# A hand-ordered opening and first turn for a two-layer graph attention kernel

## The reference

```python
# layer 0, for each graph (8 heads of 32)
nx = ln(x, ln1_g, ln1_b)
q, k, v = nx @ wq + bq, nx @ wk + bk, nx @ wv + bv
bias = where(adj > 0, 0.1 * edge * adj, -inf)          # edge is adj itself
attn = softmax(q k^T / sqrt(32) + bias)
x1 = x + (attn v) @ wo + bo
x2 = x1 + gelu(ln(x1, ln2_g, ln2_b) @ w1 + b1) @ w2 + b2   # hidden 1024, exact gelu
# layer 1, for each graph (one head of 256)
sc = (x2 @ Wq)(x2 @ Wk)^T / sqrt(256), -inf where adj == 0
y = x2 + softmax(sc) (x2 @ Wv) @ Wo + bo
out = ln(y, gamma, beta)
```

## Time and profile before

| | us |
|---|---|
| median of 3 runs (lowest, highest) | 935.13 (934.89, 935.47) |
| the profiled execution's own time | 935.03 |
| its span, first to last instruction | 933.3 |
| TensorE busy in the span | 903.3 |
| VectorE, ScalarE, GpSimd busy | 691.0, 641.2, 388.6 |
| mean granted TensorE clock | 0.993 |

### The profile page before, as it was taken

One profiled execution on the slowest core, in us unless ns is written; L12 is line 12 of the kernel. 1 busy time (PEld: TensorE's weight loads), 2 busy tenths in 40 slices (PEclk: granted clock), 3 DMA queues, 4 the chain that ended last, 5 costly groups with the idle time before them and its releaser, 6 DMA issues.

```text
span 933.3 us, 22588 instructions
## 1 busy us (share of the span) xinstructions
PE 903.3 (97%) x7623; PEld 805.8 (86%) x7623; DVE 691.0 (74%) x2576; ACT 641.2 (69%) x1888; POOL 388.6 (42%) x257
## 2 busy tenths in 40 slices
PE   8889999999999999999999999999999999998995
PEld 8677798988889898888989888898988889898894
DVE  7676877869587786958779595877968687786745
ACT  5675958668496766858677585866758586685751
POOL 3425153543616354262535526263451626344221
PEclk9999999999999999999999999999999999999998
DMA  7101000010101001010100101010010100000001
GB/s 260 35 1 35 2 24 24 30 29 0 56 0 34 22 22 34 0 51 6 34 22 22 34 0 35 22 34 22 22 34 0 34 22 28 11 24 1 24 1 34
DMA packets 29727, 26.29 MB, mean 28 GB/s; under 512 B 1126, under 2 KB 29436, under 8 KB 29692
## 3 DMA queue, kind: packets, MB, share of 16 engines
q1 hardware_dynamic: 29676, 25.83, 8.8%
q10 hardware_dynamic: 16, 0.00, 0.0%
HBM read 17.44 MB, written 8.39 MB: 28 GB/s over the span
## 4 chain that ended last, share of the span: by engine, by line
PE 43%; issue 21%; DVE 15%; POOL 14%; ACT 6%; POOLq 1%; DVEq 0%; ACTq 0%
PE bank L327 10%; PE bank L329 9%; PE bank L328 9%; DVE nx L1083 4%; POOL x L1519 4%; DVE hT_lo L1009 3%; PE bank L471 3%; POOL y L1524 3%; PE bank L564 3%; PE bank L592 3%; ACT bank L829 2%; PE bank L463 2%; POOL adj_s L1468 2%; POOL bias L1477 2%; POOL rstd L1450 2%
## 5 line engine op out<-in xcount | busy, mean ns | idle before, releaser
L804 ACT ACTIVATE bank<-p_s,neg_max 128x128 f32<-128x128 f32 x512 | 182.2, 356 | 24.1 <-DVE neg_max L1112 23.9
L1450 POOL TENSOR_TENSOR rstd<-ve,minus_half 128x4 f32<-128x4 f32 (+1 forms) x51 | 54.9, 1077 | 312.8 <-DVE ve L1076 312.8
L327 PE MATMUL bank<-w_hi,hT_hi 128*128 128x256 f32 x512 | 147.4, 288 | 0.0
L329 PE MATMUL bank<-w_hi,hT_lo 128*128 128x256 f32 x512 | 144.1, 282 | 0.0
L328 PE MATMUL bank<-w_lo,hT_hi 128*128 128x256 f32 x512 | 144.1, 281 | 0.0
L1112 DVE CUSTOM_DVE_ANT_0 p_s<-bank,bias 128x128 f32<-128x128 f32 x512 | 112.5, 285 | 8.4 <-PE bank L463 8.3
L327 PE MATMUL bank<-n2T_hi,w_hi 128*128 128x512 f32 (+1 forms) x272 | 110.1, 405 | 3.4 <-DVE qk_lo L1010 3.3
L829 ACT ACTIVATE bank<-bank,vec_cols 128x512 f32<-128x512 f32 (+1 forms) x136 | 86.6, 637 | 30.5 <-PE bank L329 30.5
L329 PE MATMUL bank<-n2T_hi,w_lo 128*128 128x512 f32 (+1 forms) x272 | 104.0, 382 | 0.0
L328 PE MATMUL bank<-n2T_lo,w_hi 128*128 128x512 f32 (+1 forms) x272 | 103.8, 382 | 0.0
L327 PEld LDWEIGHTS bank<-w_hi,hT_hi 128*128 128x128 f32 x512 | 96.4, 188 | 2.5 <-DVE hT_lo L1009 0.8
(11 more groups left out here) (211 smaller groups left out, 2460.4 us busy)
## 6 DMA issues: line engine op xcount, KB each, us to landing
xs<-in_x SPq DMA_DIRECT2D x15, 512.0 KB, 3.7
out<-y SPq DMA_DIRECT2D x15, 512.0 KB, 2.9
adj_i<-in_adj SPq DMA_DIRECT2D x15, 256.0 KB, 2.8
x2T_f<-in_L_gnn_w SPq DMA_DIRECT2D x1, 512.0 KB, 7.0
tT<-in_L_gnn_w SPq DMA_DIRECT2D x1, 512.0 KB, 7.8
y<-in_L_gnn_w SPq DMA_DIRECT2D x1, 512.0 KB, 6.4
vo<-in_L_gnn_w SPq DMA_DIRECT2D x1, 512.0 KB, 7.8
x_bo<-in_x SPq DMA_DIRECT2D x1, 256.0 KB, 2.8
```

The lines of the kernel that those rows point to most:

```text
L327: mm(out, a_hi, b_hi, start=first, stop=False)
L329: return mm(out, a_lo, b_hi, start=False, stop=last)
L804: last = run(bank[r][:, NODES * place:NODES * place + NODES], p_s[:, r, place, :], ACT.Exp, scale=-1.0, bias=neg_max[:, r, place:place + 1 ...
L1450: P.tensor_tensor(t["rstd"][:, 0:k], t["ve"][:, 0:k], minus_half[:, 0:k], ALU.pow).then_inc(ln_pool[n], 1)
```

## The change

All three engines get an order of their own for the opening, and `first_turn` in place of `turn(2, 1, 0)`. No arithmetic operation is added or dropped; `l1_product` is cut into its two halves (4 matmuls each). The hidden tiles of group 0 stand two in a bank (`up_place`), and ScalarE and VectorE take them in the order 0, 2, 1, 3, 4, 6, 5, 7 (`hidden`), a tile only once both of its bank are written. `HIGH` and `LOW` number the split weights in the order in which ScalarE and VectorE now finish them. The banks of `nx`, `n2`, `v` and the layer 1 transposes change for groups 0 and 1, and the waits with them. GpSimd's and SyncE's lists are not touched.

```diff
+        def hidden(g, i):
+            return (0, 2, 1, 3, 4, 6, 5, 7)[i] if isinstance(g, int) and g == 0 else i
+        def up_place(g, j):
+            if isinstance(g, int) and g == 0:
+                return bank[up_bank[j // 2]][:, D * (j % 2):D * (j % 2) + D]
+            return bank[at("up", g)[j % 4]][:, toks(g)]
...
+            def gelu(g, i):
+                j = hidden(g, i)
+                if isinstance(g, int) and g == 0:
+                    act.wait_ge(pe_up, 2 * (j // 2) + 2)
+                    if j % 2:
+                        act.wait_ge(dve_h, i - 1)
...
# project_v: bank 6 for both pairs of group 1
+                if isinstance(g, int) and g == 1:
+                    pe.wait_ge(*((act_k, 4), (dve_h, 7))[q])
# mlp_up of group 0
+                    if j == 4:
+                        pe.wait_ge(act_v, 2)
+                    elif j == 6:
+                        pe.wait_ge(dve_lo, LOW["qk1"])
...
# TensorE, the opening
             shift_bo()
+            norm_transpose(1)
             shifts_up()
-            l1_transpose(0)
-            norm_transpose(1)
-            l1_transpose(1)
-            p_transpose(0, 0)
-            attend(0, 0)
-            l1_transpose(2)
-            out_project(0, 0)
             project_k(1, 0)
             project_k(1, 1)
-            n2_transpose(0, False, False)
+            l1_transpose(0)
+            p_transpose(0, 0)
+            l1_transpose(1)
+            attend(0, 0)
             project_q(1, 0)
+            out_project(0, 0)
             project_q(1, 1)
+            l1_product(0, 0)
             scores(1, 0)
             project_v(1, 0)
-            project_v(1, 1)
-            l1_product(0)
-            turn(2, 1, 0)
+            n2_transpose(0, False, False)
+            l1_product(0, 1)
+            first_turn()
...
# TensorE, first_turn
+                pe.wait_ge(dve_lo, LOW["w1"])
+                for j in range(HT):
+                    mlp_up(0, j, True)
+                p_transpose(1, 0)
+                attend(1, 0)
+                out_project(1, 0)
+                l1_transpose(2)
+                scores(1, 1)
+                project_v(1, 1)
+                pe.wait_ge(dve_lo, LOW["w2"])
+                mlp_down(0, 0)
+                norm_transpose(2)
+                l1_product(1, 0)
+                l1_product(1, 1)
+                project_v(2, 0)
+                x2_transpose(0)
+                project_k(2, 0)
+                p_transpose(1, 1)
+                project_k(2, 1)
+                attend(1, 1)
+                t_project(0)
+                out_project(1, 1)
+                project_q(2, 0)
+                project_q(2, 1, True)
+                scores1(0, True)
+                scores(2, 0)
+                n2_transpose(1, True, True)
+                pe.wait_ge(dve_s1, 1)
+                project_v(2, 1)
+                vo_project(0, 0, True)
+                p1_transpose(0)
+                attend1(0)
...
# ScalarE, the opening
             exps(0, 0, 0)
             v_copy(0, 0)
-            for r in range(1, HPT):
-                exps(0, 0, r)
+            exps(0, 0, 1)
+            nxT_copy(1)
+            exps(0, 0, 2)
+            exps(0, 0, 3)
+            k_copy(1, 0)
+            k_copy(1, 1)
             pT_copy(0, 0, 0)
-            nxT_copy(1)
             pT_copy(0, 0, 2)
+            l1_copy(0, "wq1")
             l1_copy(1, "wk1")
             attn_high(0, 0)
             high_w1()
-            l1_copy(2, "wv1")
-            high_w2()
-            k_copy(1, 0)
-            k_copy(1, 1)
-            n2T_copy(0)
             q_copy(1, 0)
             q_copy(1, 1)
+            high_w2()
             exps(1, 0, 0)
+            n2T_copy(0)
+            layer1_high(0)
             exps(1, 0, 1)
             v_copy(1, 0)
-            v_copy(1, 1)
             exps(1, 0, 2)
             exps(1, 0, 3)
-            layer1_high(0)
...
# ScalarE, first_turn
+                gelu(0, 0)
+                pT_copy(1, 0, 0)
+                pT_copy(1, 0, 2)
+                gelu(0, 1)
+                gelu(0, 2)
+                attn_high(1, 0)
+                for j in range(3, HT):
+                    gelu(0, j)
+                run(probe[:, :], minus_half[:, 0:1], ACT.Exp)
+                v_copy(1, 1)
+                exps(1, 1, 0)
+                exps(1, 1, 1)
+                nxT_copy(2)
+                exps(1, 1, 2)
+                layer1_high(1)
+                exps(1, 1, 3)
+                x2T_copy(0)
+                x2T_high(0)
+                pT_copy(1, 1, 0)
+                pT_copy(1, 1, 2)
+                v_copy(2, 0)
...
+                exps1(0)
+                n2T_copy(1)
+                exps(2, 0, 0)
+                v_copy(2, 1)
+                exps(2, 0, 1)
+                vo_copy(0)
+                p1T_copy(0)
+                exps(2, 0, 2)
+                exps(2, 0, 3)
...
# VectorE, the opening
             moments(1, 1)
+            low_wo()
             biased(0, 0, 0)
             shift_v()
-            for r in range(1, HPT):
-                biased(0, 0, r)
+            biased(0, 0, 1)
+            norm1(1)
+            biased(0, 0, 2)
+            biased(0, 0, 3)
             shift_bo()
-            low_wo()
-            norm1(1)
-            divided(0, 0, 0)
+            nxT_low(1)
             shifts_up()
-            divided(0, 0, 1)
-            divided(0, 0, 2)
-            divided(0, 0, 3)
+            for r in range(HPT):
+                divided(0, 0, r)
             pT_copy(0, 0, 1)
             pT_copy(0, 0, 3)
-            l1_copy(0, "wq1")
-            nxT_low(1)
+            low_w1(0)
             attn_low(0, 0)
-            low_w1(0)
+            low_w1(1)
             residual1(0, 0, False)
             sums2(0, 0)
             moments(2, 0)
+            low_w2(0)
             norm2(0)
-            low_w1(1)
+            biased(1, 0, 0)
+            biased(1, 0, 1)
             n2T_low(0)
-            for r in range(HPT):
-                biased(1, 0, r)
-            divided(1, 0, 0)
-            low_w2(0)
-            divided(1, 0, 1)
-            divided(1, 0, 2)
-            low_w2(1)
-            divided(1, 0, 3)
-            l1_low(0, "qk1", qk1_p, SCALE1)
-            turn(2, 1, 0, None)
+            l1_low(0, "qk1", qk1_p, SCALE1)
+            biased(1, 0, 2)
+            biased(1, 0, 3)
+            low_w2(1)
+            first_turn()
...
# VectorE, first_turn
+                divided(1, 0, 0)
+                divided(1, 0, 1)
+                sums1(2)
+                divided(1, 0, 2)
+                divided(1, 0, 3)
+                moments(1, 2)
+                h_low(0, 0)
+                pT_copy(1, 0, 1)
+                pT_copy(1, 0, 3)
+                h_low(0, 1)
+                h_low(0, 2)
+                attn_low(1, 0)
+                h_low(0, 3)
+                h_low(0, 4)
+                residual1(1, 0, True)
+                sums2(1, 0)
+                l1_copy(2, "wv1")
+                for j in range(5, HT):
+                    h_low(0, j)
+                biased(1, 1, 0)
+                norm1(2)
+                for r in range(1, HPT):
+                    biased(1, 1, r)
+                residual2(0, 0)
+                divided(1, 1, 0)
+                nxT_low(2)
+                divided(1, 1, 1)
+                l1_low(1, "vo1", vo1_p, 1.0)
+                divided(1, 1, 2)
+                x2T_low(0)
+                divided(1, 1, 3)
+                pT_copy(1, 1, 1)
+                pT_copy(1, 1, 3)
...
```

More of the change, by code:

```diff
@@ L368, in shift_bo @@
                 for t in range(KT):
-                    last = mm(bank[4][:, 0:D], bv_cols[:, t, :], raw["wo"][:, t, :], start=(t == 0), stop=(t == KT - 1))
+                    last = mm(bank[5][:, 0:D], bv_cols[:, t, :], raw["wo"][:, t, :], start=(t == 0), stop=(t == KT - 1))
                 last.then_inc(pe_shift, 1)
@@ L389, in l1_transpose, with l1_product @@
                 last.then_inc(pe_l1, 1)
-            def l1_product(k):
+            def l1_product(k, m):
                 if k == 0:
+                    pe.wait_ge(act_l1, 2)
+                else:
                     pe.wait_ge(dve_l1, 1)
[L394 to L397, removed]
                 n, rhs = (("wq1", l1_T["wk1"]), ("wv1", raw["wo1"]))[k]
[L399 to L403, removed]
+                for c in range(KT):
+                    last = mm(bank[l1_mm_bank[k]][:, D * m:D * m + D], l1_T[n][:, c, 128 * m:128 * m + 128],
+                              rhs[:, c, :], start=(c == 0), stop=(c == KT - 1))
+                if m == KT - 1:
+                    last.then_inc(pe_l1_mm, 1)
             def norm_transpose(g):
-                if isinstance(g, int) and g == 1:
-                    pe.wait_ge(act_v, 1)
-                    pe.wait_ge(dve_shift, 8)
+                if isinstance(g, int) and g == 2:
+                    pe.wait_ge(act_v, 3)
                 pe.wait_ge(ln_dve[1], ln_end(g))
@@ L435, in project_q @@
```

(27 more changed lines are left out.)

104 lines of the change are left out of this document (56 added, 48 removed).

## The result

The changed kernel takes 942.62 us (median of 4 executions, 942.08 to 944.96), the kernel before 935.18 on the same chip: a ratio of 1.0084, 95% interval 1.0067 to 1.0102. It is slower, as forecast, but by 7.4 us and not by 2.4, and the time lies outside the range that I gave.

What follows compares the result with a forecast made beforehand. TensorE, busy 97% of the span, bounds the kernel; only the second turn's start can move. Opening and first turn shift it from 96.40 to 98.8 us, +2.4 on 935.03: median forecast 937.5 us, range 932.4 to 939.8.

Steps and rivals of the forecast that it cites:

- The order of the low part of the first weight ahead of `attn_low`: Opening, VectorE: `low_w1(0)` waits for `high_w1` with `attn_low(0, 0)` queued behind; TensorE stands 3.35 us ahead of `out_project(0, 0)`.
- the wait for `qk_lo`: First turn: TensorE's 3.3 us wait ahead of the fourth hidden tile goes, with about 1.6 us of slow matmuls.
- the two tiles in a bank: First turn: ScalarE waits 0.7 us for the second tile before the first `gelu`, hidden by the table load: nothing.
- the moved `low_wo`: Opening: `low_wo` fits in VectorE's 1.5 us wait for the first scores, needing 0.7 us: nothing.
- the load of group 2's `x`: First turn: it lands at about 51 us, `sums1(2)` reads it at 52.9; a cover 2 us thin.
- 1.1 us (`v(1, 1)`): First turn: `v(1, 1)` waits for low parts of hidden tiles queued behind `residual1`, `sums2` and an `l1_copy`: 1.1 us.
- 2.1 (`attend1`): End of first turn: two `exps` and a `v_copy` precede `vo_copy` and `p1T_copy`; `attend1(0)` waits 2.1 us instead of 0.4.
- I take the fall, lasting as long as the one at 52 us: Behind the wait ahead of `out_project(0, 0)`: half clock for some 3.4 us, costing 1.5 us more.
- Rival 3: A further clock fall between 42.9 and 47.8 us slows the tiles and transposes; with late `x`, 939.5 us; chance 0.12.
- Rival 2: First turn: eight tiles cover the softmax, saving 2.8 us of waits, and 1.5 with a held clock: 933.2 us; chance 0.18.

Runs made afterwards that it cites:

- a2: The changed kernel with 12 matmuls on the identity, into an unread bank, in the wait ahead of `out_project(0, 0)`: ratio 1.0044 to the kernel before.
- the repeat: The changed kernel unedited, measured and profiled a second time with more executions: ratio 1.0079 to the kernel before; the profiled execution took 940.71 us.
- b1: The kernel before with `low_w1(0)` ahead of `attn_low(0, 0)` on VectorE, nothing else: 941.09 us, ratio 1.0063.
- a6: The changed kernel with `attn_low(0, 0)` before `low_w1(0)`, `low_w2(0)` later, `vo_copy(0)`, `p1T_copy(0)` before `exps(2, 0, 1)`, `exps(1, 1, 2)` before `nxT_copy(2)`: ratio 1.0016.
- a7: a6 with VectorE's four `divided(1, 0, .)` in one piece, the `w2` splits and `sums1(2)` behind them, `h_low` right behind `residual1`: 934.21 us, ratio 0.9966.
- a9: a7 with `low_w1(0)` put back ahead of `attn_low(0, 0)` on VectorE, nothing else: 936.97 us, ratio 1.0001.

## Why the prediction was right or wrong

**What held.** What bounds the kernel: everything lies ahead of the second turn. The middle is untouched but for 0.9 us that came back behind the second turn's transposes; the earlier trace rows allowed for 2.2 there. The order of the low part of the first weight ahead of `attn_low` is the largest single price: the wait was forecast at 3.35 us and is 3.20, and the start of `out_project` after the first scores at 22.2 and is 22.9. Removed and free, as forecast: the wait for `qk_lo`, the two tiles in a bank, the moved `low_wo`, the load of group 2's `x`. The waits that I priced at 1.1 us (`v(1, 1)`) and 2.1 (`attend1`) measured 1.0 and 2.0. Ahead of the first hidden tile the forecast left TensorE 3.6 us without work (42.9 to 47.8, less 1.3), and it had 3.0 (0.89 and 2.15). Where the clock did as I assumed, up to `attend(1, 0)`, the count was short by 0.7 us of 45; 0.4 of it is `k(1)`, which had the clock at half for 3.4 us (24.3 to 27.7) where I had 2.6.

**What failed is one step, the number of falls.** "I take the fall, lasting as long as the one at 52 us" gives the sum one fall behind a wait, that ahead of `out_project(0, 0)`; every other wait is priced at its own length, as if none could bring the clock down. That fall came, and two came behind it that have no term in the sum. The missing 5.1 us (942.6 less 937.5) are, by the table: 0.8 in the start of the first scores; 0.7 up to `attend(1, 0)`; 1.5 more up to `mlp_down`, with the twelve `wo` matmuls at half clock (62.03 to 64.54) and, on the way, ScalarE's last `gelu` waiting 3.3 us for `h_low(0, 5)` behind that late residual; 1.8 more up to the second turn, of which 1.1 to `q(2, 1)` is in small parts that I can't name one by one, and 0.4 is `attend1` at half clock; 1.2 in the second turn's first tiles; less 0.9 given back. What the two falls cost can be read against a2, whose profile has neither: 9.9 us against 8.7 from `attend(1, 0)` to `mlp_down`, 1.2 against 0.8 in `attend1`, 7.0 against 5.8 from there to the transposes. That is 2.8 us. The other 2.4 us up to the transposes are my count, short nearly everywhere, where the prediction allowed it 1.2 either way. Rival 3, a further fall, was the right mechanism with the wrong place (ahead of the first tiles, where the tiles hide it, as a2 and the second profile show). Its 0.12 was little: both profiles of the changed kernel have a costly fall at a later wait.

**Why the falls are many.** The kernel before has one long wait (3.3 us) and short ones around it. The changed kernel has seven of 1.0 to 3.2 us. With the first of them filled and the order as it was (a2) about half of the loss is gone; the repeat shows that which wait brings the clock down changes from one execution to the next with the waits themselves fixed. That more waits mean more falls is what these runs suggest; none of them varies the number of waits alone. The Trainium skill (TensorE: Matmul & The Clock Gate, "What's actually happening") has this as windows that run free of the kernel; the two profiles of one kernel, a 3.2 us wait with a fall behind it and without one, agree.

**The start.** 0.8 us of the difference between the two profiled executions is ahead of anything that the change touches, and the clock is at full there in both. Over the fourteen profiles of this study the first scores start between 13.07 and 16.0 us. Ten of them lie at 13.07 to 13.89, the changed kernel's two at 13.89 and 13.09; what sets these 0.8 us stays open. The other four have a fall ahead of the first scores that begins at 9.2 to 10.3 us: 3.4 us of it in b1, a6 and a7, whose first scores start at 14.9 to 15.0, and 6.8 us in a9, at 16.0. The profile of before happened to be the earliest of all. A forecast made from one profile has that added on one side.

**The gains that I had put against it.** Rival 2, that eight tiles in a row cover the softmax, needs `divided(1, 0, 3)` ahead of the tiles' end. In the changed kernel the last division ended 2.1 us after it (57.3 and 55.3), with `low_w2(1)` and `sums1(2)` in the chain as its counter-argument said; a7 takes them out of the chain, and with the other edits it is 3.2 us faster than the kernel before by its ratio, 4.1 by the fastest executions (930.82 and 934.95). So the idea of the change is sound, and three of its orders undo it: `low_w1(0)` ahead of `attn_low(0, 0)`, the splits of `w2` and `sums1(2)` ahead of the divisions, and an `exps` ahead of `vo_copy` and `p1T_copy`.

## What to carry to other kernels

In a list that an engine issues in order, put what nobody waits for yet (here the splits of weights that the next stage needs) behind what somebody waits for: a wait for another engine's long copy is inherited by everything queued behind it. When several waits of one to three microseconds take the place of one, price the clock's falls for the set and widen the range on the slow side: here the row at hand showed two falls, the changed kernel's two profiles four and three, 3.4 to 6.8 us long, and the executions of one set lay up to 4.6 us apart. Check the start of the first untouched piece of work before reading a difference of a microsecond between two profiles.

## What the runs showed that I had not expected

Executions of one kernel lie on steps that go with the mean granted clock: the kernel before at 934.9 to 935.6 us with 0.992 or 0.993, at 936.3 to 937.7 with 0.990 to 0.992, and at 939.5 to 939.6 with 0.987; a7 from 930.82 at 0.995 to 935.35 at 0.990. A fall can be free: at half speed for 3.4 us of the hidden tiles (49.4 to 52.8 in the second profile), it left `attend(1, 0)` 10.1 us behind the first tile, against 10.0 at full clock.
